# Key roots ahead of query roots in a block's fourth section, query normalisation inside the gradient, and a 10, 10, 10, 2 spread of token scatters

## The reference

```python
def step(carry, inp):
    W, bb = carry
    xq_c, xk_c, xv_c = inp
    lr = jax.nn.sigmoid(jnp.einsum('bhkc,hcd->bhkd', xk_c, theta) + tb)
    eta = token_eta * (BASE_LR * lr / HD)
    Z1 = xk_c @ W + bb
    mu = Z1.mean(-1, keepdims=True)
    std = jnp.sqrt(Z1.var(-1, keepdims=True) + EPS)
    x_hat = (Z1 - mu) / std
    grad_output = g * x_hat + be - (xv_c - xk_c)
    gxh = grad_output * g
    grad_x = (HD * gxh - gxh.sum(-1, keepdims=True) - x_hat * (gxh * x_hat).sum(-1, keepdims=True)) / (HD * std)
    Wn, bn = W - einsum(eta * xk_c, grad_x), bb - (eta * grad_x).sum(-2, keepdims=True)
    Zq = xq_c @ Wn + bn
    out = xq_c + g * ((Zq - mu2) / std2) + be      # mu2, std2: mean and deviation of Zq
    return ((Wn, bn), out)
```

```python
top_scores, top_idx = jax.lax.top_k(scores, TOP_K)
hdn = jax.nn.gelu(jnp.einsum('th,ehf->etf', xf, w1) + b1[:, None, :], approximate=False)
y = jnp.einsum('etf,efh->eth', hdn, w2) + b2[:, None, :]
routed = jnp.einsum('te,eth->th', comb, y)
```

## Time and profile before

| | us |
|---|---|
| median of 3 runs | 672.65 (671.05 to 672.88) |
| profiled execution, its own time | 677.79 |
| span of the profiled execution | 676.0 |
| PE busy | 608.3 (90%) |
| PE weight load busy (beside PE) | 401.9 (59%) |
| DVE busy | 421.8 (62%) |
| ACT busy | 299.7 (44%) |
| POOL busy | 265.8 (39%) |
| granted TensorE clock, mean | 0.952 of full speed |

### The profile page before, as it was taken

One profiled execution on the slowest core, in us unless ns is written; L12 is line 12 of the kernel. 1 busy time (PEld: TensorE's weight loads), 2 busy tenths in 40 slices (PEclk: granted clock), 3 DMA queues, 4 the chain that ended last, 5 costly groups with the idle time before them and its releaser, 6 DMA issues.

```text
span 676.0 us, 13563 instructions
## 1 busy us (share of the span) xinstructions
PE 608.3 (90%) x5423; PEld 401.9 (59%) x5423; DVE 421.8 (62%) x779; ACT 299.7 (44%) x580; POOL 265.8 (39%) x235
## 2 busy tenths in 40 slices
PE   3999999999999996869299999999999999999586
PEld 1445544444345653645156877877778877767475
DVE  1432352543243276959395796987786987688893
ACT  1434435435435451514145645664645664645102
POOL 1080000003000147781843064686275685245421
PEclk9999799999799998869699999999999999999789
DMA  7990000000000001010241421541521541200301
GB/s 243 311 198 16 1 1 0 16 0 0 16 1 0 16 9 46 18 33 4 84 142 55 143 62 34 177 135 41 181 68 37 173 135 53 91 21 10 129 5 60
DMA packets 37405, 46.71 MB, mean 69 GB/s; under 512 B 9688, under 2 KB 22640, under 8 KB 36960
## 3 DMA queue, kind: packets, MB, share of 16 engines
q1 hardware_dynamic: 35072, 41.17, 20.7%
q0 software_dynamic: 2272, 4.69, 2.1%
HBM read 36.33 MB, written 9.51 MB: 68 GB/s over the span
## 4 chain that ended last, share of the span: by engine, by line
PE 72%; DVE 11%; POOL 8%; issue 3%; another core or an unknown queue 2%; ACT 2%; DMA 0%; POOLq 0%; SPq 0%; ACTq 0%; DVEq 0%
PE ps L882 9%; PE ps L823 8%; PE ps L835 8%; PE ps L985 7%; PE ps L956 4%; PE ps L993 4%; PE ps L948 4%; PE ps L1051 3%; PE ps L908 3%; PE ps L1035 3%; POOL small L646 3%; PE ps L812 2%; PE ps L813 2%; PE ps L809 2%
## 5 line engine op out<-in xcount | busy, mean ns | idle before, releaser
L646 POOL TENSOR_TENSOR small<-small 128x8 f32<-128x8 f32 x32 | 53.2, 1673 | 109.5 <-DVE small L1640 109.4
L604 POOL TENSOR_TENSOR small<-small 128x4 f32<-128x4 f32 x8 | 8.8, 1099 | 196.2 <-DVE small L1456 196.2
L985 PEld LDWEIGHTS ps<-wst,work 64*64 64x64 f32 x1792 | 53.5, 139 | 31.7 <-DVE wst L1674 13.7
L985 PE MATMUL ps<-wst,work 64*64 64x64 f32 x1792 | 58.7, 226 | 15.1 <-issue 4.3
L711 POOL TENSOR_TENSOR small<-small 128x8 f32<-128x8 f32 x32 | 51.9, 1636 | 31.6 <-DVE small L1632 31.6
L823 PE MATMUL ps<-work,l 128*128 128x512 f32 x128 | 56.6, 595 | 0.0
L835 PE MATMUL ps<-work,l 128*128 128x512 f32 x128 | 56.3, 593 | 0.0
L993 PE MATMUL ps<-l,mats 64*64 64x512 f32 x224 | 37.8, 690 | 17.9 <-DVE sq L1646 17.6
L686 POOL DMA_INDIRECT ys_dram<-ybuf,slot_row x39 | 47.5, 1217 | 13.6 <-issue 7.7
L1337 ACT ACTIVATE work<-ps,b1t 128x128 f32<-128x128 f32 x156 | 44.5, 371 | 17.4 <-PE ps L948 15.6
L1296 ACT ACTIVATE work<-ps 128x512 f32<-128x512 f32 x32 | 17.7, 595 | 72.8 <-PE ps L908 72.8
(11 more groups left out here) (232 smaller groups left out, 1341.5 us busy)
## 6 DMA issues: line engine op xcount, KB each, us to landing
wtile<-in_mw SPq DMA_DIRECT2D x48, 256.0 KB, 2.9
got<-in_mw SPq DMA_DIRECT2D x30, 256.0 KB
xs_dram<-ybuf SPq DMA_DIRECT2D x1, 2600.0 KB, 20.8
xg<-xs_dram SPq DMA_DIRECT2D x10, 260.0 KB, 3.9
l<-in_h SPq DMA_DIRECT2D x2, 1024.0 KB, 7.9
got<-ys_dram SPq DMA_DIRECT2D x4, 512.0 KB, 5.5
x_sb<-in_xT SPq DMA_DIRECT2D x4, 256.0 KB, 5.0
x_dram<-x_sb SPq DMA_DIRECT2D x4, 256.0 KB, 2.4
```

What stands on the lines that cost most here:

```text
L646: pool.tensor_tensor(small[:, 240 + 8 * p:248 + 8 * p], small[:, 224 + 8 * p:232 + 8 * p], small[:, 384:392], ALU.pow).then_inc(q_r.sem, 1)
L985: mm = pe.matmul(ps[64 * b:64 * b + 64, at:at + HD], x[r, q, fr:fr + CH], w(r, b, q), start=False, stop=True, skip_group_check=True)
```

## The change

In the fourth section of blocks 0 to 2, POOL takes the key roots and the learning rates before the query roots of the second section, which stood before them. DVE multiplies by these query roots (`normalise_queries(i, 1)`) not at the section's start but inside `gradients`, behind its eighth instruction. PE and ACT do three of the section's tile steps, not one, before the query work. In block 0 the token scatters are spread 10, 10, 10 and 2 over the sections where they were 12, 12, 6 and 2, and in the third section they stand ahead of `next_tokens`, not behind it.

```diff
@@ ring of PSUM banks
             ring_pair("kt", i, 3, r_act)
-            ring_tiles(steps_of(i, 3, 0, 1))
+            ring_tiles(steps_of(i, 3, 0, 3))
             ring_pair("v", i, 1, r_act)
-            ring_tiles(steps_of(i, 3, 1, 3))
@@ POOL
                 if i == 0:
-                    rows_out((12, 12, 6, 2)[c])
+                    rows_out((10, 10, 10, 2)[c])
...
-                    if i == 0 and c == NCH - 2:
-                        next_tokens(i)
+                    if c == NCH - 1 and i < NBLK - 1:
+                        query_deviations(i, c - 2)
                     rows(i, c)
                     if c == NCH - 1:
                         query_deviations(i, c - 1)
-                    if c == NCH - 2 and 0 < i < NBLK - 1:
+                    if c == NCH - 2 and i < NBLK - 1:
                         next_tokens(i)
-                    if c < NCH - 1 and (c or i):
+                    elif c < NCH - 1 and (c or i):
                         query_deviations(*((i, c - 1) if c else (i - 1, NCH - 1)))
@@ PE
                 turn_keys(i, 3)
-                tiles(steps_of(i, 3, 0, 1))
+                tiles(steps_of(i, 3, 0, 3))
                 query_bias(i, 2)
                 turn_queries(i, 1)
                 queries_through(i, 2)
-                tiles(steps_of(i, 3, 1, 3))
@@ DVE, gradients
-            def gradients(i, c, past):
+            def gradients(i, c, past, older=None):
...
                 b = shifted(1)
+                if older:
+                    normalise_queries(*older)
                 after(a)
                 a = summed(0, 1)
@@ DVE, the sections
-                    if older[0] >= 0:
+                    later = c == NCH - 1 and i < NBLK - 1
+                    if older[0] >= 0 and not later:
                         normalise_queries(*older)
...
-                    gradients(i, c, past)
+                    gradients(i, c, past, older if later else None)
```

## The result

The changed kernel took **679.5 us** (median of 4 runs, 678.54 to 683.14) against 672.43 us before (4 runs, 671.05 to 672.88): a ratio of 1.0119, with a 95% interval of 1.0078 to 1.016. Measured once more, beside other kernels, the ratio was 1.015 (1.0096 to 1.0204). It is slower; the forecast was 668.05 us with a range of 663.5 to 673, so the time lies outside.

A forecast was written before the change was run, and what follows sets the result against it. PE was taken as the bound, busy 608.3 of 676.0 us, with POOL's order setting its 12 us stall in block 0. Terms -6.1 + 0.8 + 0.7 = -4.6 took 672.65 to 668.05 us, range 663.5 to 673.

The forecast's parts named there:

- the term of blocks 1 and 2: Fourth sections of blocks 1 and 2: moved tiles about cover the later queries; +0.7 us for both, ends -3.2 and +2.0.
- Block 0, fourth section: PE's bias products start at 331.3 instead of 337.45: -6.1 us, of which 2.5 come from the second section.
- Block 0, second and third section: Two fewer scatters ahead of the second section's query roots let the splitting start 2.5 us earlier; lower end 0.5.
- by 0.3 us, that is, just: Block 0, third section: ten scatters end at 316.6, hidden behind the target product's wait, which ends at 316.9.
- rival B: Block 0: one of the third section's ten scatters runs long, splitting starts 3.7 us later, 671.8 us in all; chance 0.14.
- Scatters beside PE: Block 0, second section's 64 query products now run beside scatters and slow down: +0.8 us, ends 0 and 6.3.
- The trickle (A): Block 0, second section: scatters hold PE's small query products, about 676 us in all, slower; chance 0.10.
- Roots that hold DVE: Each POOL root holds one DVE instruction, so normalised queries come 3.3 us later in three blocks: 678 us; chance 0.04.
- my four: Rivals: trickle of small products (0.10), one long scatter (0.14), roots holding DVE (0.04), more gain than forecast, 663.4 us (0.14).

The follow-up runs named there:

- kernel 12: The whole change, run again beside other versions, against the kernel before on the same chip: 680.17 us, ratio 1.015.
- kernel 10: Kernel before with only block 0's part (scatters, roots' order, normalisation), on the chip of the whole change's rerun: 668.14 us, ratio 0.9969.
- kernel 3: Changed kernel with the scatters of tiles 5 and 21 issued one section earlier: 671.94 us, ratio 1.0021 to the kernel before.
- kernel 4: Kernel before with only the tile steps moved ahead of the query work; roots, normalisation and token scatters as before: 679.93 us, ratio 1.0152.
- kernel 1: Changed kernel with blocks 1 and 2 in their old order, so only block 0's part: 667.56 us, ratio 0.9954 to the kernel before.
- kernel 11: Kernel before with only block 0's scatters spread 10, 10, 10, 2 and the splitting behind the third ten: 665.86 us, ratio 0.9922.
- kernel 9: Kernel before with only block 0's key roots ahead of the query roots and query normalisation inside the gradient: 674.47 us, ratio 1.0067.
- kernel 6: Block 0's part alone, with scatters spread 10, 10, 6, 6, on chip II: ratio 0.9984 to the kernel before.
- kernel 7: Kernel before with only block 0's scatters spread 10, 10, 10, 2 ahead of the splitting, on chip II: ratio 0.9878.
- kernel 5: Kernel before with the tile steps moved and the scatters of tiles 5 and 21 one section earlier, chip II: 687.21 us, ratio 1.0034.

## Why the prediction was wrong

**The step that failed** is the term of blocks 1 and 2: "So the moved tiles about pay for the moved queries, no more. Two blocks: +0.7", with ends of -3.2 and +2.0. Measured, it is 680.17 - 668.14 = **+12.0 us** on one chip (kernels 12 and 10), and +6.1 and +6.0 in the profile. (Kernel 12's profile has blocks of 107.3 and 102.7 us, not 106 each; its slow stretches were 13.7 and 6.8 us long.) I followed the moved tiles through PE, where they are 4.26 us of work, and allowed ACT's gelus 0.6 each; I did not list what else the moved steps issue or wait for. Each tile step also holds a copy on ACT with a wait for the slot of eight tiles earlier, which is POOL's scatter behind both pairs of roots. Moved ahead, this wait stands in front of the bank that PE needs for the queries. Kernels 3 and 4 show it from both sides: with the wait taken away most of the loss goes, and with the tiles moved and nothing else blocks 1 and 2 are nearly as long (105.2 and 105.6 us). The clock made it dearer: 2.2 us more idle time in the stretch went with 3.7 us of slower products in block 1. The slow stretch of block 1 began before the wait for the copy, and was 10.2 us long with that wait and 3.4 without it (kernel 3); block 2 had one of 10.2 us with that wait and none without it.

The trace of before could have told it. These are POOL's scatter of tile 5 and ACT's copy of tile 13 in its block 1:

```profile
446.72 1.18 POOL L686 DMA_INDIRECT ys_dram<-ybuf,slot_row  x1 [0.39 <-POOL slot_share L681]
```

```profile
449.69 0.39 ACT L1347 ACTIVATE ybuf<-ps,slot_share 128x128 f32<-128x128 f32 x1
```

The copy starts 2.97 us after the scatter. In the changed trace, where it waited, it was let go 2.42 us after the scatter's start (437.42 to 439.84). So there was a margin of 0.55 us, and the change took the copy 5.6 us forward against the splitting of the tokens (it was ready 5.40 us after the splitting's end, 434.03 - 428.63, and before it came 449.69 - 438.69 = 11.00 us after it), while the scatter stays behind both pairs of roots.

**The rest of that term** was right where it could be seen: the wait for the queries was 2.13 and 2.08 us (1.9 predicted), and in block 2 of kernel 3 the price was 0.4 us, where 0.35 was predicted. I left out that an idle time of 2.1 us, half a microsecond more than before, can be followed by the lower clock: it was in block 1 of kernel 3, where slower products cost 1.5 us, and was not in block 2. Of kernel 3's 4.4 us over kernel 1, 2.0 are in neither block. In the profiles block 3, which has the same order in both, is 3.0 us longer at a lower clock, as it is in kernel 11 against kernel 10; what brings that on stays open.

**Block 0, fourth section** (-3.6 of the -6.1): right to a tenth. From the splitting to PE's bias products I had 14.4 us and it was 14.43, and DVE's new wait for the query squares is 4.34 us where I had 4.8 (POOL, behind it, idles the 5.08 us shown above). But that sum hid two terms of opposite sign, -7.6 for the six scatters and +4.0 for the key roots going first, and I never asked what the second is for. Kernels 9 and 11 are the answer: it is 2.3 us better without it by the medians, 3.2 by the ratios.

**Block 0, second and third section** (-2.5, lower end 0.5): the gain was right and the cover was not. The target product came 3.1 us earlier (79.3 us after the block's first product, against 82.4). But from that first product to the splitting it is 82.6 us in the changed kernel and 82.4 in kernel 9, which has the old spread; nothing was left. One of the ten scatters of the third section took 4.88 us, the splitting stood 3.2 us behind the target product, and the hiding "by 0.3 us, that is, just" had no room for it. It is rival B, which I gave 0.14; it came in every trace with this spread. With it (3.7 us) block 0 would have been -6.1 + 0.8 + 3.7 = -1.6; kernels 1 and 10 gave -3.1 and -2.1 by the ratios (-4.3 and -3.8 by the medians) for block 0.

**Scatters beside PE** (+0.8): the 64 query products of the second section took 2.39 us in the changed trace against 1.96, 0.4 more. But their first 1.10 us ran at the lower clock. In kernel 12 the same products, at the full clock and with two scatters beside them, took no longer than elsewhere, so on this chip the scatters cost nothing:

```profile
296.43 1.91 PE L984 MATMUL ps<-wst,work 64*64 64x64 f32 x64
```

The trickle (A) came neither there nor in the changed trace; on chip II a mild form of it did (kernels 6 and 7). **Roots that hold DVE** (C): the eight gradient instructions from 321.24 to 326.3 lie beside POOL's roots and took 0.68 or 0.69 us each, two inputs in SBUF or not:

```profile
323.30 0.68 DVE L1685 TENSOR_TENSOR l<-ps,small 128x512 f32<-128x512 f32 x1
323.90 0.68 DVE L1696 TENSOR_TENSOR sq<-l 128x512 f32<-128x512 f32 x1
324.50 0.68 DVE L1689 TENSOR_TENSOR l<-l,gg 128x512 f32<-128x512 f32 x1
```

The Trainium skill (SBUF — State Buffer, Who interferes with whom) would have the third of these wait out a root; this trace does not agree.

**The missing rival.** None of my four was a wait for a buffer's slot. The Trainium skill (PSUM — Partial Sum Buffer, Engine vs sequencer instructions) calls ScalarE's queue strictly first in, first out, and the trace agrees, with 5.81 us of idle time ahead of tile 13's copy, and the copy of the turned tokens, ready at 434.18, done only behind it at 440.20. I had applied that order to DVE and POOL and not to ACT.

## What to carry to other kernels

When a group of steps moves, list for every engine each instruction that moves and each semaphore that it waits for, buffer slots that come round included. An engine with much idle time can hide such a wait until the order changes: here it was ACT, busy for 44% of the span before. If a change has two parts with one sum, price each by itself: here the scatters alone bring 5 to 7 us, the roots' order in block 0 costs 2 to 5, and the moved tiles with the roots' order of blocks 1 and 2 cost 12. And cover of 0.3 us under a run of transfers is none, if one transfer in ten is five times as long.

## What the runs showed of the hardware

**With ten scatters in a section, every tenth is long.** Scatters of tokens take 0.96 us as a rule, with 0.30 between. In the changed trace three of the 32 took 4.9 us; by count they are the 6th, the 16th and the 26th:

```profile
276.93 4.89 POOL L671 DMA_INDIRECT xs_dram<-wtile,pos  x1 [0.30 <-issue]
```

(the others begin at 253.32 and at 303.11). Kernels 10 and 11 have them at the same three places by count, of 4.90 to 4.97 us. With the old spread (before, and kernels 4, 5 and 9) only the 6th was above 3 us, but the elementwise instruction that POOL ran next after the 16th was long instead: 4.01 us in the kernel before, 4.33 and 4.34 in kernels 4 and 9, 2.56 in kernel 5, against 0.5 to 0.8 with ten to a section. The cause is not shown.

```profile
283.46 4.01 POOL L661 TENSOR_SCALAR wtile<-row_of 128x16 f32<-128x16 f32 x1 [1.77 <-DMA xs_dram<-wtile,pos]
```

**Short stalls can cost as much again.** Idle times of 2.1 us on PE in front of the bias products stand in six places of three traces (blocks 1 and 2 of the changed kernel and of kernels 3 and 12). In five the granted clock fell to 1.2 GHz, between 0.2 us before their end and 1.6 us after it; in block 2 of kernel 3 it did not fall, nor after the 1.58 us of before in either block. Where a wait for the copy followed, the slow stretch was 6.8 to 13.7 us long; where none did, 3.4. In block 1 of the changed kernel 2.2 us more idle time went with 3.7 us of slower products.
